# A graph attention kernel: three key/value buffers instead of two in the attention pass

## What is computed

```python
h = relu(layernorm(x)); n1 = layer_norm(h) * g1 + b1
q, k, v = n1 @ Wq + bq, n1 @ Wk + bk, n1 @ Wv + bv        # 12500 x 8 x 16 each
# over all edges and one self loop per node:
e = sum(q[dst] * k[src], -1) / sqrt(16)
p = exp(e - segment_max(e, dst)[dst]); z = segment_sum(p, dst)
agg = segment_sum(p / z[dst] * v[src], dst)               # 0 for nodes without an edge
x = x + (h + agg @ Wo + bo, then x + mlp(layer_norm(x)))  # MLP 128 -> 512 -> 128, exact gelu
h = relu(layernorm(x))
x = x + mlp1((1 + eps) * h + segment_sum(h[src], dst))
```

## Time and profile before

| | us |
|---|---|
| median of 3 runs (lowest, highest) | 4827.98 (4821.74, 4830.42) |
| profiled execution, device time | 4826.0 |
| profiled execution, span from first to last instruction | 4824.4 |
| VectorE busy in the span | 2847.1 (59%) |
| ScalarE busy in the span | 2136.2 (44%) |
| GpSimd busy in the span | 3407.3 (71%) |
| TensorE busy in the span | 507.4 (11%) |

### The profile page before, as it was taken

One profiled execution on the slowest core, in us unless ns is written; L12 is line 12 of the kernel. 1 busy time (PEld: TensorE's weight loads), 2 busy tenths in 40 slices (PEclk: granted clock), 3 DMA queues, 4 the chain that ended last, 5 costly groups with the idle time before them and its releaser, 6 DMA issues.

```text
span 4824.4 us, 22224 instructions
## 1 busy us (share of the span) xinstructions
PE 507.4 (11%) x2377; PEld 356.6 (7%) x2377; DVE 2847.1 (59%) x4386; ACT 2136.2 (44%) x2140; POOL 3407.3 (71%) x3610
## 2 busy tenths in 40 slices
PE   4620000000000000000189000000000000000007
PEld 2410000000000000000067000000000000000004
DVE  7837999999999999999778222222222222222223
ACT  4414555454444555554367344444444444444432
POOL 4677777777777777777554677777777777777766
PEclk8655555555555555555599555555555555555558
DMA  9995666666666666666455233333333333333334
GB/s 360 381 370 182 218 211 212 214 214 216 214 213 214 214 214 216 211 211 210 151 119 125 93 102 101 101 105 102 104 104 104 104 104 104 104 104 104 104 98 138
DMA packets 235483, 816.46 MB, mean 169 GB/s; under 512 B 67005, under 2 KB 93789, under 8 KB 185242
## 3 DMA queue, kind: packets, MB, share of 16 engines
q1 hardware_dynamic: 77464, 457.58, 25.5%
q0 software_dynamic: 143232, 344.58, 25.0%
q10 hardware_dynamic: 14722, 13.70, 0.9%
HBM read 455.00 MB, written 354.21 MB: 168 GB/s over the span
## 4 chain that ended last, share of the span: by engine, by line
POOL 42%; issue 19%; DVE 15%; DMA 10%; DVEq 7%; PE 5%; ACT 1%; SPq 0%; POOLq 0%; ACTq 0%
POOL arena L635 41%; DMA q_edges<-arena 7%; DVE ps L1689 4%; DMA arena<-kv_tab,idx 2%; DVE ps L1735 2%; DVE arena L1682 2%; PE ps L1322 2%; PE ps L1311 2%; DVE arena L1751 2%; DVEq L1706 2%; DVEq L1776 2%; DVEq L1718 2%; DVE ps L1631 1%; DVEq L1723 1%; DVE ps L1713 1%
## 5 line engine op out<-in xcount | busy, mean ns | idle before, releaser
L635 POOL DMA_INDIRECT arena<-h_tab,idx x1568 | 1479.7, 944 | 520.4 <-issue 500.1
L635 POOL DMA_INDIRECT arena<-kv_tab,idx x1568 | 1482.6, 946 | 506.9 <-issue 493.5
L1927 DVE SCALAR_TENSOR_TENSOR ps<-arena,keep,ps 128x128 f32<-128x128 f32 x97 | 42.4, 438 | 1486.4 <-ACT ps L1193 1486.4
L1193 ACT COPY ps<-arena 128x2048 f32<-128x2048 f32 x97 | 347.9, 3587 | 768.1 <-DMA arena<-h_tab,idx 768.1
L1206 ACT COPY arena<-arena 128x2048 f32<-128x2048 f32 x97 | 354.2, 3652 | 402.2 <-DVE arena L1934 402.2
L1631 DVE TENSOR_TENSOR_SCAN ps<-arena,ps 128x256 f32<-128x256 f32 (+2 forms) x584 | 502.4, 860 | 0.3
L1058 ACT COPY arena<-arena 128x1024 f32<-128x1024 f32 x196 | 375.4, 1915 | 176.7 <-DVE arena L1751 176.7
L1751 DVE TENSOR_TENSOR_SCAN arena<-arena,ps 128x1024 f32<-128x1024 f32 x196 | 445.5, 2273 | 7.6 <-issue 0.4
L1934 DVE TENSOR_TENSOR_SCAN arena<-arena,ps 128x1024 f32<-128x1024 f32 x194 | 433.0, 2273 | 7.5 <-issue 0.4
L1047 ACT COPY ps<-arena 128x1024 f32<-128x1024 f32 x196 | 363.3, 1886 | 10.1 <-DMA arena<-q_edges 4.0
L1042 ACT COPY arena<-keep 128x960 f32 (+1 forms) x99 | 98.2, 992 | 463.5 <-DVE arena L1751 446.3
(11 more groups left out here) (249 smaller groups left out, 2450.8 us busy)
## 6 DMA issues: line engine op xcount, KB each, us to landing
states<-arena SPq DMA_DIRECT2D x98, 1152.0 KB, 5.4
q_edges<-arena SPq DMA_DIRECT2D x98, 1024.0 KB
arena<-q_edges SPq DMA_DIRECT2D x98, 1024.0 KB, 7.7
states<-arena SPq DMA_DIRECT2D x98, 1024.0 KB, 4.1
arena<-kv_tab,idx POOLq DMA_INDIRECT x1568, 2.8
arena<-h_tab,idx POOLq DMA_INDIRECT x1568, 2.5
kv_tab<-arena ACTq DMA_DIRECT2D x14, 896.0 KB, 9.5
arena<-kv_tab SPq DMA_DIRECT2D x14, 448.0 KB, 5.7
```

What stands on the lines that cost most here:

```text
L635: pool.indirect_dma_start(to, None, tab, bass.IndirectOffsetOnAxis(ap=at, axis=0)).then_inc(done, 16)
L1193: nc.scalar.copy(rows_now, rows[k].rearrange("p b f -> p f b")).then_inc(rows_turned, 1)
```

## The change

A third key/value buffer is added, `kvb` has KV_BUFFERS = 3 entries, and batch n uses buffer n modulo 3, with three landing semaphores `kv_in`. `idx` stays at two buffers. GpSimd waits for `weighed_s` of batch n - 3 instead of n - 2. Since its loop has to know both n modulo 3 and n modulo 2 when the program is built, the loop body now covers KV_TURN = 6 batches: batches 1 to 5 are written out, the loop covers batches 6 to 95 in 15 turns, and 96 and 97 are written out. The tiles behind the buffers move up by 4096 floats. VectorE's instructions are the same, with other addresses and another semaphore to wait for.

```diff
+KV_BUFFERS = 3
+KV_TURN = 2 * KV_BUFFERS
...
-        kvb = cB.two(B, 2 * HID)
+        kvb = [cB.take(B, 2 * HID) for _ in range(KV_BUFFERS)]
...
-        q_in, kv_in, states_out = sem2("q_in"), sem2("kv_in"), sem2("states_out")
+        q_in, states_out = sem2("q_in"), sem2("states_out")
+        kv_in = [sem(f"kv_in{t}") for t in range(KV_BUFFERS)]
...
-            def batch_b(i, first):
-
-                for k in range(2):
-                    n = i * 2 + k
-                    if first and k == 0:
-                        continue
-                    pool.wait_ge(idx_set, n + 1)
-                    if not first:
-                        pool.wait_ge(weighed_s, n - 1)
-                    settle(pool)
-                    for b in range(B):
-                        gather(kvb[k][:, b, :], kv_tab, idx[k][:, b:b + 1], aside_in if last_batch(n) and b < BH else kv_in[k])
-            repeat(pool, BPAIRS, batch_b, tail=1)
+            def batch_b(n, m):
+
+                pool.wait_ge(idx_set, n + 1)
+                if not (isinstance(n, int) and n < KV_BUFFERS):
+                    pool.wait_ge(weighed_s, n - KV_BUFFERS + 1)
+                settle(pool)
+                for b in range(B):
+                    gather(kvb[m % KV_BUFFERS][:, b, :], kv_tab, idx[m % 2][:, b:b + 1],
+                           aside_in if last_batch(n) and b < BH else kv_in[m % KV_BUFFERS])
+            for n in range(1, KV_TURN):
+                batch_b(n, n)
+            with pool.Fori(1, BATCHES // KV_TURN) as i:
+                for m in range(KV_TURN):
+                    batch_b(i * KV_TURN + m, m)
+            for n in range(BATCHES // KV_TURN * KV_TURN, BATCHES):
+                batch_b(n, n)
...
-                keys = kvb[n % 2][:, b0:b1, 0:HID]
+                keys = kvb[n % KV_BUFFERS][:, b0:b1, 0:HID]
...
-                                        kvb[n % 2][:, b0:b1, 0:HID].rearrange("p b (h d) -> p b h d", d=HD), AX.X, ALU.add)
+                                        kvb[n % KV_BUFFERS][:, b0:b1, 0:HID].rearrange("p b (h d) -> p b h d", d=HD), AX.X, ALU.add)
...
-                dve.wait_ge(kv_in[k], n // 2 * BW + BW - (16 * BH if last_batch(n) else 0))
+                dve.wait_ge(kv_in[n % KV_BUFFERS], n // KV_BUFFERS * BW + BW - (16 * BH if last_batch(n) else 0))
...
-                values = kvb[n % 2][:, :, HID + half * HF:HID + half * HF + HF]
+                values = kvb[n % KV_BUFFERS][:, :, HID + half * HF:HID + half * HF + HF]
```

## The result

| | before | after |
|---|---|---|
| median of 6 runs each, us (lowest, highest) | 4825.81 (4821.74, 4830.42) | 4796.09 (4792.13, 4799.85) |
| span of the profiled execution, us | 4824.4 | 4796.2 |

The ratio is 0.9938, 95% interval 0.9925 to 0.9950: some 30 us less.

What follows compares the result with a forecast made beforehand. GpSimd's gather issue was taken to bound pass B, with VectorE close behind. Batch 2's earlier start gave 1.45 us, all other terms 0: 4828.0 - 1.5 = 4826.5 us, range 4816 to 4836, no change that can be told.

Steps and rivals of the forecast that it cites:

- What bounds the kernel, and the sum of pass B: Pass B: GpSimd's issue sets it; 96 batches at 20.01 us make 1921.0 of 1947.5 us, long gaps the other 26.5.
- the 12 long gaps: GpSimd's pass B, every 112th gather: 2.3 to 3.2 us instead of 0.30, together 26.5 us, expected to stay.
- The wait for a free buffer: Pass B, batch 2's first gather: the only place this wait bound; the third buffer saves 1.45 us, bounds 0 to 1.76.
- With 12 or 13 long gaps 112 gathers apart.: Sign that the forecast is right: pass B keeps its long gaps at this spacing; it is wrong if they vanish.
- The first rival: Pass B: the third buffer lets VectorE run at its own pace, or removes the long gaps; both forms together 0.05.
- smaller form: Pass B's long gaps come from a buffer that is not free; 26.5 us go, 4801.5 us; both forms together 0.05.
- larger form: Pass B: GpSimd gets ahead and VectorE never waits; 35 us go, 4793 us; both forms together 0.05.
- The loop over six batches: GpSimd's pass B: 15 turns instead of 47 and a body of about 117 instructions against 39; taken as 0 us.
- The warning that the Trainium skill gives for taken branches: GpSimd's loop end: a branch outside the two held pages stalls for a fetch; costed 0, the body lying within them.
- the cover of 35 us: VectorE in pass B: 0.10 us a batch faster than GpSimd, so it could grow by 35 us in all before costing time.

Runs made afterwards that it cites:

- e3: The changed kernel with GpSimd's passes B and D written out for all 98 batches, without a loop; 4796.60 us.
- e7: The changed kernel with three landing semaphores in pass D (still two row buffers), GpSimd's passes B and D and ScalarE's D written out; 4774.75 us, ratio 0.9892.
- e8: The changed kernel with two landing semaphores in pass B, four in pass D (two row buffers), those passes written out; 4800.29 us.
- e9: Against the kernel before: pass B two buffers, three landing semaphores; pass D three row buffers, two semaphores; passes written out; 4805.40 us.
- e2: The changed kernel, but GpSimd waits for the weighed values of batch n - 2 as before, and pass D loops over four batches; 4799.49 us.
- e1: The kernel before (two key/value buffers), but with GpSimd's loops over six batches in passes B and D; 4824.91 us.
- e6: Against the kernel before: pass B two buffers, four landing semaphores; pass D three row buffers, three semaphores; written out; 5374.39 us, kernel before 5340.85 beside it.
- e4: The kernel before with three landing semaphores in passes B and D, buffers still two, GpSimd's passes written out; 5352.51 us, kernel before 5340.85 beside it.

## Why the prediction was wrong

- *What bounds the kernel, and the sum of pass B.* Right for the kernel before: GpSimd's issue set pass B. The sum took one batch's 20.01 us for all and so had 26.5 us left for the 12 long gaps; read one by one they are 27.8 us over the usual 0.30 each, and an ordinary batch 20.00 us. After, it is 19.99 us a batch and no gap.
- *The wait for a free buffer.* Right in place and size: batch 2's gap of 1.76 us is 0.30 after. It is 1.45 us of the 30. Batch 2 still began at 408.62 us, not near 407.5, because the gather ahead of it came 1.15 us later in that execution (407.37 against 406.22); in e3 and e7 batch 2 begins at 407.1.
- *"With 12 or 13 long gaps 112 gathers apart."* This is the step that failed. I took the gaps for a property of the count of gathers and left their 26.5 us standing on both sides of the sum, because pass D has them at the same spacing "with other buffers and another partner engine". That comparison held one thing fixed that the change moves: pass D, too, counts its landings on two semaphores. The runs put nearly the whole of the error there: with the third buffer in place, three semaphores instead of two are worth 27.5 us in pass B (e7 against e8), and with two buffers 23 us in B (e9) and 24 us in D (e7).
- *The first rival.* Its smaller form priced the gaps at 26.5 us and the time at 4801.5, with a chance of under 0.05. The price was nearly right and the cause was not: "a buffer that is not free". My ground against it was that the gap comes at the second gather, when the wait for the buffer has passed. That is true, and e8 confirms it, but it argues only against the buffer. The larger form had VectorE never wait, 4793 us; measured are 4796.09 us and 4.5 us of waiting. Its size was nearer than any other, though the lead came from the gaps that went and not from a buffer in hand. The parts of the prediction never cost the third landing semaphore, though the diff names it.
- *What the third buffer itself is worth.* The early wait cost 3.4 us from batch 2 on in e2 (1922.6 against 1919.2), and the gap ahead of batch 2 another 1.4. In e9, with two buffers, the gap of batch 2 and the short gaps add 3.1 us over the usual 0.30. Of that 1.2 us are the gap of batch 2, forecast at 1.45; the rest is what the fixed stop of the sequencer costs when it is let go only 2.2 us ahead of need. With the late wait that stop lies behind the queued gathers.
- *The loop over six batches.* Right: nothing, with no stop at a turn's end, and e3 without a loop takes the same 4796.6 us. The warning that the Trainium skill gives for taken branches ("Runtime: NRT & Kernel Launch", "Instruction fetch mechanics") found no case here: the instruction queue moved 58 packets after against 57 before, 26 against 24 of them from 500 to 2300 us, and no gap stands at a turn's end.
- *VectorE.* Half right. Its work did not grow: the median from one batch's keys to the next is 19.92 us after, against 19.91 read before. But the cover of 35 us, held to be spare, was what the lost gaps drew on: 4.5 us of waiting are left. By that, a further gain on GpSimd alone in pass B has at most these 4.5 us to win, an estimate that was not tried.

## What to carry to other kernels

When a stall at a regular distance has no releaser, list all that the stalled and the unstalled stretches share before calling it fixed, semaphores included. Here GpSimd's indirect DMAs, issued back to back on two alternating landing semaphores, cost 1.8 to 2.9 us over the usual gap every 112 gathers, and a third semaphore took that away without any memory. Where an edit adds a buffer, try its semaphore alone first, and look at which engine comes next: here VectorE had only 35 us to follow with.

## What the runs showed of the hardware

- GpSimd's sequencer stops at intervals in a stream of indirect DMAs: every 112 gathers with two landing semaphores used in turn for 16 gathers each, 96 with three, 80 with four. These three spacings are 128 less 16 for each semaphore beyond the first; what is counted, and whether it is to 128, the traces don't say.
- With two semaphores no gather after a stop started before those in flight had landed, whatever the lead: 2.0 to 3.4 us of idle engine (before, after, e1), also with some 12 gathers queued (pass D, where the sequencer is 14.9 us ahead of the engine). With three the stop has a fixed length of 2.35 us of the sequencer (e2), and a full queue hides it. With four it is 0.37 us shorter (3.25 against 3.62 us from the release, e6 and e4).
- Why two semaphores drain and three or four don't was not found. Each semaphore took 16 gathers in a row in every run; another split was not tried.
